# A first stage and attention in one program block, with attention's opening steps among the last output products, and two unsplit fp32 gate products

## The reference

```python
# 1: a state-space block, whose convolved input is replaced by ones
xc, z = split(norm(x) @ W_in.T)
xc = silu(conv(xc)) * 0 + 1
dBC = xc @ W_x.T
delta = softplus(dBC[..., :64] @ W_dt.T + b_dt)      # A = -exp(A_log)
h = exp(delta * A) * h + delta * B * xc              # scan over the 512 rows
y = h . C + D_skip * xc
x = x + (y * silu(z)) @ W_out.T
# 2: cross attention of norm(x) to the context, 16 heads, causal mask; x = x + attn @ Wo + bo
# 3: a shared expert and the top 2 of 8 experts (gelu, 256 -> 1024 -> 256); x = x + their sum
```

## Time and profile before

| | us |
|---|---|
| median of three runs | 964.97 (964.14 to 967.13) |
| the profiled execution | 969.2 |
| its span, first to last instruction | 967.4 |
| TensorE busy | 911.7 |
| VectorE, ScalarE, POOL busy | 596.1, 522.2, 339.8 |

### The profile page before, as it was taken

The page is one execution under the profiler, slowest core; times in us unless marked ns, Lnnn a source line. Parts: engine busy times, 40 slices in busy tenths (PEclk is TensorE's granted clock), DMA queues, the critical chain, the costliest instruction groups (busy, mean ns, idle before and its releaser), DMA issues.

```text
span 967.4 us, 20474 instructions
## 1 busy us (share of the span) xinstructions
PE 911.7 (94%) x7054; PEld 805.9 (83%) x7055; DVE 596.1 (62%) x1437; ACT 522.2 (54%) x1057; POOL 339.8 (35%) x318
## 2 busy tenths in 40 slices
PE   5799986899998989999999999999999999999996
PEld 5679984466565668888889899999999999999996
DVE  5988566667755676666656467556464656565453
ACT  3584312655544644555644466565575757565552
POOL 3549202211211155555555143324343332432222
PEclk9999998999999989999999999999999999999999
DMA  8300002000002011111124652524334342523222
GB/s 252 93 1 1 2 1 93 1 2 2 1 1 70 27 47 69 63 63 63 63 74 162 204 131 46 143 45 126 51 65 115 78 100 38 141 39 51 45 45 33
DMA packets 48943, 64.01 MB, mean 66 GB/s; under 512 B 9984, under 2 KB 41920, under 8 KB 48768
## 3 DMA queue, kind: packets, MB, share of 16 engines
q0 software_dynamic: 17504, 34.87, 15.6%
q1 hardware_dynamic: 31248, 27.46, 9.7%
q10 hardware_dynamic: 144, 1.05, 0.4%
HBM read 38.59 MB, written 24.77 MB: 66 GB/s over the span
## 4 chain that ended last, share of the span: by engine, by line
PE 73%; DVE 7%; ACT 3%; issue 1%; DMA 0%; POOL 0%; SPq 0%; DVEq 0%; POOLq 0%; ACTq 0%
PE PS L135 21%; PE PS L136 20%; PE PS L137 20%; PE PS L797 3%; DVE mxpad L1048 2%; PE PS L1710 2%; PE PS L838 2%; PE PS L824 2%; PE PS L844 1%; ACT recs L953 1%; ACT prT L934 1%; PE PS L1260 1%; DVE mxT L1059 1%; DVE hidl L141 0%; PE PS L805 0%
## 5 line engine op out<-in xcount | busy, mean ns | idle before, releaser
L1756 ACT ACTIVATE hideh<-PS,be 128x256 fp32r<-128x256 f32 x280 | 140.6, 502 | 152.2 <-PE PS L137 152.2
L1784 POOL DMA_INDIRECT out_rows<-y,toki x70 | 123.9, 1770 | 265.0 <-DVE y L1824 255.0
L141 DVE TENSOR_TENSOR hidel<-act32e,hideh 128x256 fp32r<-128x256 f32 x280 | 118.5, 425 | 107.8 <-ACT act32e L1758 107.3
L135 PE MATMUL PS<-xTeh,wfch 128*128 128x256 f32 x560 | 159.4, 285 | 2.1 <-issue 1.1
L136 PE MATMUL PS<-xTel,wfch 128*128 128x256 f32 x560 | 158.5, 283 | 0.0
L137 PE MATMUL PS<-xTeh,wfcl 128*128 128x256 f32 x560 | 158.4, 283 | 0.0
L135 PE MATMUL PS<-wprh,hideh 128*128 128x256 f32 x560 | 157.9, 282 | 0.0
L137 PE MATMUL PS<-wprh,hidel 128*128 128x256 f32 x560 | 154.8, 277 | 0.0
L136 PE MATMUL PS<-wprl,hideh 128*128 128x256 f32 x560 | 154.8, 277 | 0.0
L1758 ACT ACTIVATE act32e<-PS,be 128x256 f32<-128x256 f32 x280 | 140.9, 503 | 2.8 <-DVE hidel L141 2.8
L135 PEld LDWEIGHTS PS<-xTeh,wfch 128*128 128x128 f32 x560 | 107.3, 192 | 3.7 <-issue 2.6
(11 more groups left out here) (272 smaller groups left out, 2119.1 us busy)
## 6 DMA issues: line engine op xcount, KB each, us to landing
xr<-routed_rows SPq DMA_DIRECT2D x36, 272.0 KB, 2.8
fcraw<-in_Wfc POOLq DMA_DIRECT2D x8, 1024.0 KB, 5.8
prraw<-in_Wproj POOLq DMA_DIRECT2D x8, 1024.0 KB, 8.4
X<-in_x SPq DMA_DIRECT2D x8, 512.0 KB, 6.5
out_rows<-X SPq DMA_DIRECT2D x8, 512.0 KB, 2.9
routed_rows<-pads SPq DMA_DIRECT2D x8, 272.0 KB, 4.4
out_rows<-y,toki POOLq DMA_INDIRECT x70, 3.8
ctx<-in_ctxT SPq DMA_DIRECT2D x4, 256.0 KB, 6.6
```

Source lines behind the costliest of these rows:

```text
L135: nc.tensor.matmul(out, wh, xh, start=first, stop=False)
L141: return eng.tensor_tensor(out, whole, high.bitcast(F32), ALU.subtract)
L1756: nc.scalar.activation(hid[0][:, j, :], PS[:, j % 4, 0:BLK], ACT.Gelu_apprx_tanh, bias=bias)
L1784: nc.gpsimd.indirect_dma_start(out=out, out_offset=bass.IndirectOffsetOnAxis(ap=toki[:, h:h + 1], axis=0), in_=y[:, h, :], in_offset=None, ...
```

## The change

1. Both stages are now functions, and one block runs them: attention's lists call the first stage's (`first[0]` to `first[4]`) and hand their opening steps in, to be placed among its last ones. The meeting of the engines between the stages is gone.
2. Batches 0 and 1 (`WHOLE = 2`) take z from one fp32 matmul per product, of win and a whole hT that ScalarE copies. VectorE no longer makes hTl for them, and it makes winl later, after the statistics of batch 3.
3. The opening's transposes stand behind bo's matmuls and use banks 0 and 1, the queries of batches 0 and 1 banks 2 and 3. The rows of the first scores stand between the halves of the last output product. Where a bank has an old use a wait is added.
4. SP's loads of attention are issued inside the first stage: sel and the mask after the small matmuls, the shared expert's weights after output products 5 and 6. gh's second buffer and bvc lie elsewhere.

The diff without its changes of indent, cut:

```diff
+            WHOLE = 2
...
-                    sp.wait_ge(late_in, LATE_IN)
+                sp.wait_ge(small_mm, 2)
+                small_loads()
+                sp.wait_ge(o_psum, 2 * 6)
+                up_load()
+                sp.wait_ge(o_psum, 2 * 7)
+                down_load()
...
+                def rows_split(b):
+                    if b < WHOLE:
+                        pe.wait_ge(hT_high, KD * b + KD)
+                    else:
+                        pe.wait_ge(hT_low, KD * (b - WHOLE) + KD)
...
                     def z_part(b, parts=range(KE)):
-                        pe.wait_ge(hT_low, KD * b + KD)
+                    rows_split(b)
+                    if b == WHOLE:
+                        pe.wait_ge(win_split, 2)
...
+                            if b < WHOLE:
+                                last = nc.tensor.matmul(PS[:, e, :], win[:, k, e * P:(e + 1) * P], hT[:, b, k, :],
+                                                        start=k == 0, stop=k == KD - 1)
+                            else:
                                 last = product(PS[:, e, :], [w[:, k, e * P:(e + 1) * P] for w in winp],
...
-                    pe.wait_ge(win_split, 2)
+                pe.wait_ge(win_in, 16)
...
+                out_part(B - 4)
                     pe.wait_ge(bv_ready, 1)
+                pe.wait_ge(z_copied, KE * B)
                     for k in range(KD):
-                        last = nc.tensor.matmul(PS[:, 0, 0:D], bv[:, k, :], wo[:, k, :], start=k == 0, stop=k == KD - 1)
+                    last = nc.tensor.matmul(PS[:, 2, 0:D], bv[:, k, :], wo[:, k, :], start=k == 0, stop=k == KD - 1)
                     last.then_inc(bo_psum, 1)
+                first_rows()
+                out_part(B - 3)
+                first_queries()
+                out_part(B - 2)
+                pe.wait_ge(k_ready, KD * B)
+                first_scores(0)
+                out_part(B - 1, range(0, 2))
+                first_scores(1)
+                second_rows(0)
+                out_part(B - 1, range(2, TB))
+                first_scores(2)
+                second_rows(1)
+                first_scores(3)
...
-                    x_low(0)
...
-                    x_low(1)
...
                     stats_part(3)
+                dve.wait_ge(win_split, 1)
+                low(nc.vector, winp[1][:], win[:], winp[0][:]).then_inc(win_split, 1)
                     columns(0)
...
+                round_start(3)
                             for half in hn_ready:
                                 dve.wait_ge(half, B)
                             norm_stats(link, tiles(0)).then_inc(hn_var, 1)
...
+                first_rows()
+                gate(7)
...
+                gate_low(6)
+                first_queries()
+                residual(5)
+                gate_low(7)
+                second_rows()
+                residual(6)
+                first_maxima()
+                residual(7, range(0, 1))
+                third_maxima()
+                residual(7, range(1, 2))
...
+                high(5)
+                act.wait_ge(late_in, LATE_IN)
+                first_rows()
+                high(6)
+                high(7)
+                first_queries()
...
             def x_bank(b, i):
-                return 7 if b == 0 and i == 1 else 6
+                return i if b < 2 else 6
+
+            def q_bank(b, m):
+                return 2 + m if b < 2 else QB[m]
...
                     elif b:
                         pe.wait_ge(o_divided, b)
+                    else:
+                        pe.wait_ge(qT_ready, 2 * KD)
```

More of the change, by code:

```diff
@@ new lines, in z_part, with kernel_sums @@
+                        last.then_inc(z_psum, 1)
+                def kernel_sums(half):
+                    pe.wait_ge(cU_ready, 2 * half + 2)
+                    if half:
+                        pe.wait_ge(ksb_ready, half)
+                    for q in range(GH // 2):
+                        for j in range(2):
+                            g = GH * j + GH // 2 * half + q
+                            last = nc.tensor.matmul(PS[NB * j:NB * (j + 1), 6 + q // 8, q % 8 * NB:(q % 8 + 1) * NB],
+                                                    powers[:, g, 0:NB], cU[:, g, :], start=True, stop=True,
+                                                    skip_group_check=True)
+                    last.then_inc(raw_psum, 1)
@@ new lines, in out_part @@
+                def out_part(b, part=range(TB)):
+                    if b == 0:
+                        pe.wait_ge(wout_split, 2)
+                    pe.wait_ge(g_low, b + 1)
+                    for t in part:
+                        if b and t % 2 == 0:
+                            pe.wait_ge(x1_ready, 2 * (b - 1) + t // 2 + 1)
+                        for e in range(KE):
+                            at = e * L + t * P
+                            last = product(PS[:, 6 + t // 2, (t % 2) * D:(t % 2 + 1) * D],
+                                           (gh[b % 2][:, at:at + P], gl[:, b % SLOTS, at:at + P]),
+                                           [w[:, e, :] for w in wouts], e == 0, e == KE - 1)
+                        if t % 2:
+                            last.then_inc(o_psum, 1)
@@ new lines, in first_tensor @@
+                pe.wait_ge(w_in, W_IN)
+                pe.wait_ge(ones_ready, 1)
+                for k in range(KE):
+                    nc.tensor.matmul(PS[0:R, 6, 0:1], wx[:, k, 0:R], ones[:, 0:1],
+                                     start=k == 0, stop=k == KE - 1)
+                for k in range(KE):
+                    last = nc.tensor.matmul(PS[:, 7, 0:2 * NS], ones[:, :], wx[:, k, R:R + 2 * NS],
+                                            start=k == 0, stop=k == KE - 1)
+                last.then_inc(small_mm, 1)
@@ new lines, in first_tensor, with z_and_transposes @@
+                pe.wait_ge(consts_in, 32)
+                transposes(0)
+                pe.wait_ge(dlt_ready, 1)
+                for e in range(NE):
+                    last = nc.tensor.matmul(PS[0:G, 6, 8 + e:9 + e], wdt[:, e, :], dlt[:], start=True, stop=True)
+                last.then_inc(small_mm, 1)
+                pe.wait_ge(win_in, 16)
+                def z_and_transposes(b):
+                    z_part(b, range(KE - 1))
+                    transposes(b + 1)
+                    z_part(b, range(KE - 1, KE))
@@ new lines, in first_tensor @@
+                z_and_transposes(0)
+                pe.wait_ge(rates_ready, 1)
+                for i, src in enumerate((rate, coef)):
+                    last = nc.tensor.transpose(PS[:, 7, P + G * i:P + G * (i + 1)], src[:], ident[0:G, 0:G])
+                last.then_inc(small_mm, 1)
+                z_and_transposes(1)
+                kernel_sums(0)
+                z_and_transposes(2)
+                kernel_sums(1)
+                keys()
+                kernel_turn(0)
+                kernel_turn(1)
@@ new lines, in first_tensor @@
+                last.then_inc(bo_psum, 1)
+                first_rows()
[11 more added lines that the diff above has]
+                first_scores(3)
@@ L1010, in add_bo @@
                         nc.gpsimd.tensor_tensor(xs, xs, bo[:], ALU.add).then_inc(bo_added, 1)
+                first[3](pool)
                 pool.sem_inc(hn_rstd, 2)
```

929 lines of the change are left out of this document (442 added, 487 removed).

## The result

| | before | after |
|---|---|---|
| median, us | 967.13 (964.14 to 969.20, 5 runs) | 956.23 (955.02 to 959.64, 5 runs) |
| ratio | | 0.989 (0.9866 to 0.9914) |
| profiled execution, us | 969.2 | 955.0 |
| its span, us | 967.4 | 953.4 |

The change gains 10.9 us, or 8.3 to 13.0 by the interval. 14.25 were forecast. The kernel before, timed again with the changed one, came out at 967.13, not at 964.97; the changed one missed the range's upper end of 954.5 by 1.7. The two profiled spans lie 14.0 apart, as forecast (953.1 against 953.4). The profile of before is of the longest of its five executions, that of after of the shortest of its five, so the two profiles overstate the gain.

What follows compares the result with a forecast made beforehand. TensorE, busy 94% of the span, was taken as the bound, so only its idle or low-clock stretches could give. Opening 3.45 plus join 10.8 net made 14.25 us, 964.97 to 950.7; range 947.5 to 954.5.

Steps and rivals of the forecast that it cites:

- The gate product's start and VectorE's chain: Opening: gate product starts near 14.3 us, 2.1 earlier; VectorE's columns cU ready at 35.0 us, 2.15 earlier.
- The clock before the kernel sums: Opening: after 2.2 us of idle time TensorE keeps the high level, sums take 2.08 us, 1.5 us gained.
- the opening: First stage's start, up to the second kernel sums: fp32 gate products for batches 0 and 1 gain 3.45 us.
- the term with the low clock: Lower bound of the opening's gain if the clock is low again at the kernel sums: 2.15 us.
- The four passes: Opening: an fp32 product costs 0.91 us against 0.68 for three split ones, 3.6 us more over 16 products.
- The rival built on it: Opening: four passes against three make TensorE the bound, so the opening gives nothing: 954.2 us, chance 0.07.
- The join: First stage to attention: opening steps hidden among output products, fourth maxima end at 153.8 not 165.20 us, gain 11.4.
- The added wait: Before attention's first key scores: they wait for ScalarE's second query copy, charged 0.6 us, at most 0.8.
- The sum of the two terms: Opening 3.45 plus join 10.8 net gives 14.25 us, taken off the median 964.97.
- rival 1: The clock falls again before the first kernel sums: gain 2.15 + 10.8, 952.0 us, chance 0.14.
- The low end: 947.5 us: early level rise (0.7), no added wait (0.6), up to 1.3 for a low-clock stretch falling away.

Runs made afterwards that it cites:

- c2_after: The changed kernel, unedited, timed and traced once more in the same rounds as its two halves: 957.49 us, ratio 0.9897.
- e3_fill3: Changed kernel plus three unused fp32 matmuls filling TensorE's idle time before the first kernel sums: 956.45 us, ratio 0.988.
- e2_fp32_only: Kernel before plus only the new opening (fp32 gate products for batches 0 and 1, later split of W_in): 966.20 us, ratio 0.998.
- c1_before: The kernel before, unedited, timed against itself and traced again: ratio 0.9996.
- e5_behind: Changed kernel, still one block, with attention's opening steps except batch 0's norm on VectorE behind the last output product: 967.64 us, ratio 0.9985.
- e7_winl_late: e6_held with the split of W_in behind the columns cU and two extra matmuls before the kernel sums instead of three: 955.20 us, ratio 0.9849.
- e1_join_only: Changed kernel with the old opening back (split gate products, W_in split at its old place), so only the join changed: 962.05 us, ratio 0.9928.
- e9_after_hold: Changed kernel plus 11 and 10 unused matmuls in two idle stretches at the start of the shared expert: 957.22 us, ratio 0.9869.
- e6_held: Changed kernel with extra matmuls before the kernel sums and at the shared expert's start, batch 1's queries in their old banks: 954.44 us, ratio 0.9858.
- e8_high_first: e7_winl_late with ScalarE making batch 6's high part before attention's first high rows: 955.81 us, ratio 0.9848.

## Why the prediction was right or wrong

**The gate product's start and VectorE's chain: right.** It starts 2.75 us earlier, of which about 0.5 is the whole execution running ahead (the small matmuls end at 13.70 instead of 14.24); 2.2 are left, 2.1 were forecast. The columns were forecast for 35.0 and came at 34.5. In the profiled run this is partly luck, since two misses cancel: rcT came at 23.5, not 24.9 (the gate product started 0.7 us before the forecast's 14.3, and the level rose after 3.4 us, not 4.0), and the wait of 1.0 us for POOL's rstd, which the forecast took away, stayed. In c2_after the same steps came as forecast: rcT at 24.86, that wait gone, the columns at 34.80.

**The clock before the kernel sums: wrong for the profiled run, right for the next one.** The step said 2.2 us of idle time and the high level. It was 3.20 us, since TensorE was done earlier than forecast, and the level was low. In c2_after, the same program, it was 2.10 us and high. e3_fill3 shows the price, 1.2 us. How soon TensorE was done hung on when the level rose: in the fourteen traces that was 3.4 to 6.0 us after the first gate matmul, and the forecast took one value, 4.0. Counted at the second kernel sums, the opening gave 2.98 us in the first pair of traces, 2.85 in e2_fp32_only and 3.98 in c2_after (both against c1_before), where 3.45 were forecast and 2.15 was the term with the low clock.

**The four passes: right as a price, nearly without effect.** A fp32 product takes 0.86 to 0.90 us (blocks of 1.72 us, and 5.42 for six), near the keys' 0.91. The rule of the Trainium skill ("FP8 and Floating Point Precision", TensorE Precision Notes), four passes, holds in the trace. The rival built on it has fallen by e2_fp32_only. But batch 0's products are not off the chain: VectorE's wait for the transposes behind them, 1.17 us in c2_after, stands in that chain, and only the wait for rstd that went away with it hid all but 0.27 of it.

**The join: right.** 11.4 were forecast to the fourth maxima: 14.23 less 2.98 is 11.25. The added wait was charged 0.6 and cost 0.8. Net 10.4 against 10.8. e5_behind shows that without the overlap nothing of it is left.

**From the traces' sum to the median: this is the step that failed.** The sum of the two terms is 13.4 us in the traces and 9 to 13 us in the medians, 10.9 and, by the ratio of c2_after, 10 (8 to 12). "The median becomes 950.7" stood on two things. The first is the base: 964.97, the median of three executions, where later sets of the same kernel had 967.13, 967.88, 968.80, 969.06, 969.12 and 971.21. This alone puts 2.2 of the 5.5 us into the miss. The second is that the gain worked out in one profile was taken for that of the median: 14.25 forecast, 10.9 measured, the other 3.3 us. Of these 0.9 are the two terms, whose sum is 13.4 in the traces, and some 2.5 lie between traces and medians (more still in the second pair of traces, 14.4 us apart at weighing 0; the intervals of the medians end at 13.0 and 12.3). Both traces of the changed kernel are of the shortest execution of their sets (955.02 and 953.99, medians 956.23 and 957.49). Of chance stretches at the low clock the forecast knew, but except for the one before the kernel sums (rival 1) it let them widen only the low end of the range.

What these traces hold of such stretches, counted between 100 us and the last expert blocks: all five with two blocks, or with the opening steps behind, have one at the join (in e5_behind twice as long) and one more each, two in the first profile. The nine with the overlap have none at the first query product; elsewhere they have one to three (e7_winl_late none): at 150, at 176 to 184, at 330, at 540 us. Where the landmarks show its price, at the first three places, it is 1.2 to 1.6 us. So the changed kernel is free of one sure stretch, and which others it meets differs from execution to execution.

The stretch at 540 us stands beside a larger chance. Behind the first down product the traces take 611.4 to 616.7 us, and most of this spread arises at one place. There TensorE waits for the load of the second block of rows for the routed experts (xr), 0.86 us in c2_after and 4.23 in e1_join_only:

```profile
537.89 0.66 PE L1794 MATMUL PS<-ident,xr 128*128 128x128 f32 x4 [0.86 <-DMA xr<-routed_rows]
```

```profile
544.89 0.66 PE L1796 MATMUL PS<-ident,xr 128*128 128x128 f32 x4 [4.23 <-DMA xr<-routed_rows]
```

The load is issued at nearly the same place and lands after 3.6 us in c2_after and after 7.0 in e1_join_only; why is open. The low stretch follows in six traces, five of them with the overlap, after waits of 2.7 to 4.2 us, and all six take 614.3 us or more. The eight without it, with waits of 0.9 to 3.0 us, take 611.4 to 613.1. From weighing 0 to the end of the span the five traces without the overlap take 786.9 to 790.5 us, mean 788.1, and the nine with it 787.9 to 793.0, mean 789.8. An estimate from these means: 1.7 of the 2.5 us are lost behind weighing 0. In the first pair of profiles (788.9 and 788.3) nothing of it shows. That the change makes long waits there more frequent isn't shown; fourteen traces of twelve different kernels are few for that.

The single times say that the level of the clock has a part. For 76 single times of the kernel before the mean granted clock is known. In these, and in the 11 of the changed kernel, longer times go with a lower mean granted clock (correlation -0.73 and -0.88). The eleven have a mean clock of 0.9925, the two that were profiled 0.994 and 0.996. That chance stretches and waits are the whole 2.5 us fits the numbers but isn't shown: taking away one place (e9_after_hold) moved the time by no more than the intervals allow.

**The range and the chances.** Faster was right. The range ended at 954.5; with the base's spread of 2 us on both ends, as the three times shown ahead (964.14 to 967.13) would have allowed, it would have held 956.2. The low end was not added up right either: 950.7 less 0.7, 0.6 and 1.3 is 948.1, not 947.5. The steps that name a mechanism held; the number failed on the base and on what single profiles are worth.

## What to carry to other kernels

A chain of short steps on three engines costs little when it stands among long products of the stage before, and all of it when it stands behind them; one block for both stages without that overlap gave nothing here. In this opening fewer steps on VectorE were worth more than passes saved on TensorE. But a step moved out of a chain gives its length only as far as the next engine was waiting for it: the columns came 1.1 us sooner, what followed them 0.2 to 0.6. A forecast should start from the spread of the kernel's executions, not from a median of three, and a gain read between two profiles should be checked against which executions they are.

## What the runs showed of the hardware

TensorE's clock after an idle time of 2 to 3 us is not the same in each execution. Before the kernel sums it idled 3.20 us in one trace, and the level fell within that time. After 3.04 or 3.05 us, in four, it fell 0.1 to 0.9 us after the sums began. After 2.10 or 2.12 us it stayed high in two traces (sums of 2.08 and 2.09 us) and fell 0.7 to 1.1 us into the sums in three (2.80 to 3.12 us). Where extra matmuls filled the time (four traces) the sums took 2.09 us. Such matmuls hold the level (e3_fill3, e6_held), yet low stretches remain at other idle places: shortening VectorE's wait in e8_high_first won 1.3 us and the key scores lost 1.2. At the start the level rose 3.4 to 6.0 us after the first gate matmul, TensorE working without a pause. The low level before that rise isn't in the granted clock, which reads 1.00 from 17 to 20 us in the first profile, where the matmuls have a pitch of 0.427 us:

```profile
17.00:20.00 3.00, 3.00 (x9) 1.00 0.95 237
```

The load of the second block of rows (xr) landed after 3.6 to 7.0 us in the six traces that show its landing.
